# VectorE's order inside a tick of a fused Mamba and attention pipeline: product, maximum, scan instead of product, scan, maximum

## The chip, the cores and the metric

The kernel runs on one core of a Trainium2 chip. The metric is the device time of one execution, in microseconds (us). The time of the kernel before is 8423.08 us, the median of 3 runs (8422.37 to 8431.92).

The engines are called PE (TensorE, the matrix engine; PEld is its weight load), DVE (VectorE), ACT (ScalarE), POOL (GpSimd) and SP (SyncE, which here only issues DMAs). Each runs its own instructions in the order in which they are written; between engines there are only semaphores.

## The reference

Input x has 16 images of 64 channels and 64x64 points. Two layers follow each other:

```
y   = leaky_relu(conv2d_3x3(x, w1, b1));  y = leaky_relu(conv2d_3x3(y, w2, b2))
seq = y as 4096 steps of 64 channels
# Mamba: 128 inner channels d, 16 states n, steps one after the other
h   = exp(delta[d] * A[d, n]) * h + (delta[d] * u[d]) * B[n]
y[d] = sum_n h[d, n] * C[n]              # then + u*D, * silu(z), @ out_proj
# second layer, on x1 = output of the first
out_c = softmax(xc xc^T) x1              # channel attention, 64 x 64
attn  = softmax(q^T k)                   # spatial attention, 4096 x 4096 for each image
out   = x1 + w_bn [out_c ; v attn^T]
```

## The kernel before

**Stages.** The two 3x3 convolutions of all images come first. Then one pipeline carries everything else of all images. It is cut into ticks. An image has 8 chunks of 512 steps, and the 128 x 16 recurrences are packed as 16 groups of 128 lanes; one tick T is one group of one chunk, so there are 16 ticks (r = T % 16 = 0 to 15) in a chunk, 128 in an image and 2048 in all. While image a is scanned, the attention of image a-1 runs: from tick 122 on a search for the largest score (one pair of 128x512 tiles a tick), from tick 160 on the attention itself (one key tile of 128 against 1024 queries a tick, a quarter of the queries in 32 ticks).

**One tick, engine by engine.** A tick is the same number of instructions on each engine, plus what belongs to its r:
- SP fetches the `lanes` of tick T+3 (one 512 KB read from `spread_d`), after the product and `dA` of tick T-1.
- ACT: `relu` of the search difference into `gains` (line 952), which waits for the maximum of tick T-1; two `exp` into `pr` (line 1007); `dA` of tick T+1 (line 1013), which waits for `lanes` and for the scan of tick T-1; then the copies of its r.
- DVE: the *product* of lanes and B into the PSUM bank DBU (line 1141), which waits for the scan of tick T-1; the *scan* (line 1152), which waits for the product and for `dA`; the *maximum* (line 1093), one instruction that adds the PSUM bank of the search to `gains` and reduces it, and which waits for PE's search product of this tick and the relu of the tick before; then the extra instructions of its r, such as the convolution taps (r = 1, 2, 3), `ysb` (line 1133, ahead of the product of r = 3), gates and splits.
- PE: search difference (line 836), the scores (lines 899 and 901, twice), the search product for the maximum (line 836 again), the values of tick T-1 (line 911), every second tick the sums (line 926), and then the small products of its r. At r = 2 the small product is `y` (line 873): 32 matmuls that sum a whole chunk's 16 states.
- POOL: after the scan of T-1 it copies the last column into `carry` (line 1262), and after the product of T it multiplies the scanned `hst` by C (line 1269). At r = 4 it gates `ysb` (line 1275).

**Ring of banks.** All of PE's results but three take turns in 5 PSUM banks (`RING = 5`); a matmul waits until the result five uses back has been read. Four uses a tick and one for each small product. So the search product for the maximum waits for the *scores* of the tick before in a plain tick, and for the *maximum of the tick before* where one small product stands between:

```
if number[e] >= RING:
    taken(pe, sched.uses[number[e] - RING])
```

Every second chunk, at r = 11, PE transposes the row of maxima (`turn`); DVE reads it (line 1103) and splits it in three for the next quarter.

**What the change touches** is the body of DVE's loop over T. `small_use` issues the maximum; the scan's block is unchanged.

Of the kernel before, what the change touches and what calls it, by code (L numbers as in the profile page):

```python
# [92 lines left out]
def group_of(T):  # L93

    k = T % GROUPS
    return k % BLOCKS * GPB + k // BLOCKS


def slot_of(T):

    k = T % GROUPS
    return k if k >= HALVES or T // GROUPS % 2 == 0 else k + GROUPS
# [316 lines left out]
def pipeline(nc, banks, seq_d, scratch, w_in, cw, cb, w_dt_t, w_dt, dt_b, w_bc, a_log, skip,  # L419
# [4 lines left out]
    with ExitStack() as ctx:  # L424
# [138 lines left out]
        def span(j, images, tail, i):  # L563
# [9 lines left out]
            def due(name, event, times=1):  # L573

                return sched.counts.get(name, {}).get(event, 0) * times

            def wait(eng, name, event, times=1):

                if due(name, event):
                    eng.wait_ge(S[name], due(name, event, times))  # L580
# [6 lines left out]
            def bank_of(e):  # L587
                return RB[number[e] % RING]

            def full_wait(eng, e):  # L590

                if e in number:
                    eng.wait_ge(S["ring_full"], number[e] + 1)

            def taken(eng, e):

                if e in sched.freed:
                    eng.wait_ge(S[sched.freed[e][0]], sched.freed[e][1])
# [55 lines left out]
            with nc.Block() as block:  # L654
# [418 lines left out]
                def _(dve):  # L1073
                    steps = [0]

                    def link(ins):

                        steps[0] += 1
                        ins.then_inc(S["dstep"], 1)
                        dve.wait_ge(S["dstep"], steps[0])  # L1080

                    def small_use(e):
                        kind, c = e[0], e[1]
                        if kind not in DVE_USES or kind == "y":
                            return
                        full_wait(dve, e)
                        bank = bank_of(e)
                        if kind == "max":
                            k = e[2]
                            taken(dve, ("dif", c, k))  # L1090
                            if k == 0:
                                wait(dve, "max_in", sched.before(c))
                            nc.vector.tensor_tensor_reduce(  # L1093
                                out=gains[:, k % 2, :], in0=bank[:], in1=gains[:, k % 2, :], scale=1.0,
                                scalar=LOWEST, op0=ALU.add, op1=ALU.max,
                                accum_out=mxp[:, k % NT, k // NT:k // NT + 1]).then_inc(S["dve_took"], 1)
                            if k == KT - 1:
                                taken(dve, e)
                                nc.vector.tensor_reduce(mx[:], mxp[:], AX_X, ALU.max).then_inc(S["max_in"], 1)
                        elif kind == "turn":  # L1100

                            wait(dve, "nm_row", sched.before(c), 48)
                            nc.vector.tensor_scalar(nmx[:, 0, :], bank[0:NT, 0:P], -1.0, None,
                                                    ALU.mult).then_inc(S["dve_took"], 1)
                            taken(dve, e)
                            link(nc.vector.tensor_copy(nm3[:, 0, :], nmx[:, 0, :]))
                            link(nc.vector.tensor_tensor(nmx[:, 1, :], nmx[:, 0, :], nm3[:, 0, :], ALU.subtract))
                            link(nc.vector.tensor_copy(nm3[:, 1, :], nmx[:, 1, :]))
                            nc.vector.tensor_tensor(nm3[:, 2, :], nmx[:, 1, :], nm3[:, 1, :],
                                                    ALU.subtract).then_inc(S["nm3_in"], 1)  # L1110
                        elif kind == "mix":

                            nc.vector.tensor_tensor(mixw[0:CH, 0:CH], bank[0:CH, 0:CH], ident[0:CH, 0:CH], ALU.add)
                            nc.vector.tensor_tensor(mixw[CH:P, CH:P], bank[CH:P, 0:CH], ident[CH:P, CH:P],
                                                    ALU.add).then_inc(S["dve_took"], 1)
                        elif kind == "res":
                            nc.vector.tensor_tensor(accs[:], accs[:], bank[:], ALU.add).then_inc(S["dve_took"], 1)
                        elif kind == "en":
                            if c % CHUNKS == 0:
                                ins = nc.vector.tensor_copy(energy[:], bank[0:CH, 0:CH])  # L1120
                            else:
                                taken(dve, ("en", c - 1))
                                ins = nc.vector.tensor_tensor(energy[:], energy[:], bank[0:CH, 0:CH], ALU.add)
                            ins.then_inc(S["dve_took"], 1)

                    for T in range(first, last):
                        sl, r = T // GROUPS, T % GROUPS
                        ev = sched.small_uses(T)
# [6 lines left out]
                        if sched.scans(T):  # L1135
                            wait(dve, f"lanes{T % SLOTS}", T, 16)
                            if r == 0:
                                wait(dve, "ld_b", sl, 16)
                            if due("scan", T - 1):
                                dve.wait_ge(S["scan"], due("scan", T - 1))  # L1140
                            nc.vector.tensor_tensor(DBU[:], lanes[:, T % SLOTS, 1, :], bbc[:, sl % 2, :],  # L1141
                                                    ALU.mult).then_inc(
                                S["dbu_in"], 1)
                        if sched.scans(T):
                            g = group_of(T)
                            if due("dbu_in", T):
                                dve.wait_ge(S["dbu_in"], due("dbu_in", T))
                            if due("da_in", T):
                                dve.wait_ge(S["da_in"], due("da_in", T))
                            wait(dve, "carried", T - GROUPS)  # L1150
                            full_wait(dve, ("y", sl - 1 if T % GROUPS >= HALVES else sl - 2))
                            nc.vector.tensor_tensor_scan(  # L1152
                                hst[:, slot_of(T), :], dA[:, T % 2, :], DBU[:],
                                carry[:, g:g + 1] if sl % CHUNKS else 0.0, ALU.mult, ALU.add).then_inc(S["scan"], 1)
                        for e in ev:
                            if e[0] == "max":
                                small_use(e)
                        c = sl + 1
                        if sched.chunk(c):
                            x_ = xin[:, c % 2, :]  # L1160
# [168 lines left out]
```

## Time and profile before

| | us |
|---|---|
| median of 3 runs | 8423.08 |
| profiled execution, its own time | 8432.17 |
| its span, first to last instruction | 8430.3 |
| PE busy | 7658.1 (91%) |
| DVE busy | 6758.3 (80%) |
| ACT busy | 5963.6 (71%) |
| POOL busy | 3407.8 (40%) |
| granted TensorE clock, mean | 0.962 |

Busy time is summed over an engine's instructions. PE's is generous: a matmul of 512 columns is drawn as 0.38 us long, while the next one starts 0.22 us after it. So a small stall of PE can hide under a matmul's drawn end.

### The profile page before, as it was taken

The numbers are of one execution on the slowest core, as the hardware profiler recorded it, in microseconds if no ns is written. First come the engines' busy times: TensorE is split into PE (matmuls) and PEld (weight loads), VectorE is DVE, ScalarE is ACT, GpSimd is POOL, SyncE is SP. The second block draws the span as 40 slices with busy tenths as digits, with TensorE's granted clock in tenths as the row PEclk, the third lists the DMA queues.
The fourth block names the chain that finished last, engine by engine and source line by source line (L and its number), as shares of the span: only waits on it lengthen the run. The fifth ranks groups of instructions, "written<-read, shape, count | busy, mean of one in ns | idle before, by whom it ended". The sixth has DMA issues, their size and how long they took to land. (4 is left out here: it accounts for less than half of the span.)

```text
span 8430.3 us, 156342 instructions
## 1 busy us (share of the span) xinstructions
PE 7658.1 (91%) x48454; PEld 2321.5 (28%) x48454; DVE 6758.3 (80%) x10982; ACT 5963.6 (71%) x10582; POOL 3407.8 (40%) x4135
## 2 busy tenths in 40 slices
PE   8982389998999999989999999989999999989999
PEld 2220122222222222222222222222222222222222
DVE  2228889898989899888989898988989898989721
ACT  1114468777778788777877787877878787878754
POOL 0005544444444444444444444444444444434300
PEclk9985689999999999999999999999999999999999
DMA  8738878787787887877777878878787878778600
GB/s 130 121 80 217 216 202 202 196 200 186 195 206 193 201 202 197 197 190 195 197 196 198 207 191 201 200 181 201 200 201 196 201 192 206 197 183 202 150 26 11
DMA packets 886565, 1531.37 MB, mean 182 GB/s; under 512 B 409480, under 2 KB 459472, under 8 KB 885712
## 3 DMA queue, kind: packets, MB, share of 16 engines
q1 hardware_dynamic: 882640, 1520.79, 74.0%
q8 instruction: 389, 6.37, 0.4%
q14 instruction: 464, 3.80, 0.2%
q10 hardware_dynamic: 3072, 0.40, 0.0%
HBM read 1326.69 MB, written 176.95 MB: 178 GB/s over the span
## 5 line engine op out<-in xcount | busy, mean ns | idle before, releaser
L1269 POOL TENSOR_TENSOR hst<-hst,cbc 128x512 f32<-128x512 f32 x2048 | 2609.8, 1274 | 3664.6 <-DVE bank L1141 3642.7
L1152 DVE TENSOR_TENSOR_SCAN hst<-dA,carry,bank 128x512 f32<-128x512 f32 x1792 | 2293.8, 1280 | 94.7 <-ACT dA L1013 22.5
L1007 ACT ACTIVATE pr<-bank 128x512 f32<-128x512 f32 x4096 | 2226.6, 603 | 61.3 <-PE bank L901 59.1
L911 PE MATMUL bank<-pr,vt 128*32 128x512 f32 x16384 | 2192.5, 607 | 0.0
L952 ACT ACTIVATE gains<-bank 128x512 f32<-128x512 f32 x2048 | 1223.8, 598 | 1141.0 <-PE bank L836 748.8
L836 PE MATMUL bank<-s1kx,s1q 128*128 128x512 bf16 x4096 | 1588.2, 389 | 199.7 <-DMA s1kx<-kx_d 76.9
L1013 ACT ACTIVATE dA<-lanes,small 128x512 f32<-128x512 f32 x2048 | 1501.0, 733 | 354.7 <-DMA lanes<-spread_d 312.1
L899 PE MATMUL bank<-s1q,s1k 128*128 128x512 bf16 x4096 | 1568.2, 383 | 176.1 <-ACT pr L1007 152.5
L1141 DVE TENSOR_TENSOR bank<-lanes,bbc 128x512 f32<-128x512 f32 x2048 | 1514.9, 740 | 163.2 <-DMA lanes<-spread_d 56.7
L1093 DVE CUSTOM_DVE_ANT_0 gains<-bank,gains 128x512 f32<-128x512 f32 x2048 | 1369.7, 669 | 326.6 <-PE bank L836 319.2
L901 PE MATMUL bank<-t2q,t2k 128*128 128x512 bf16 x4096 | 1562.1, 381 | 0.0
L926 PE MATMUL bank<-pr,ones 128*32 128x512 f32 x8192 | 1069.5, 594 | 1.9 <-ACT dens L1022 1.7
L836 PEld LDWEIGHTS bank<-s1kx,s1q 128*128 128x128 bf16 x4096 | 397.6, 97 | 1779.5 <-issue 1137.0
L899 PEld LDWEIGHTS bank<-s1q,s1k 128*128 128x128 bf16 x4096 | 400.1, 98 | 710.1 <-ACT pr L1007 333.0
L873 PE MATMUL bank<-hst,cst 128*32 128x512 f32 x4096 | 484.4, 615 | 79.0 <-POOL hst L1269 79.0
L911 PEld LDWEIGHTS bank<-pr,vt 128*32 128x32 f32 x16384 | 323.7, 108 | 789.8 <-issue 777.4
L901 PEld LDWEIGHTS bank<-t2q,t2k 128*128 128x128 bf16 x4096 | 403.0, 98 | 403.4 <-issue 10.6
L1262 POOL COPY carry<-hst 128x1 f32<-128x1 f32 x1792 | 483.8, 270 | 40.3 <-DVE hst L1152 35.8
L926 PEld LDWEIGHTS bank<-pr,ones 128*32 128x32 f32 x8192 | 266.5, 111 | 626.2 <-issue 522.1
L388 ACT ACTIVATE biased<-bank,bias 128x512 f32<-128x512 f32 x128 | 80.9, 683 | 504.0 <-PE bank L376 504.0
L1133 DVE SCALAR_TENSOR_TENSOR ysb<-u,small,bank 128x512 f32<-128x512 f32 x128 | 95.6, 747 | 340.8 <-issue 324.7
L1152 DVE TENSOR_TENSOR_SCAN hst<-dA,bank 128x512 f32<-128x512 f32 x256 | 312.4, 1220 | 15.2 <-ACT dA L1013 5.4
(116 smaller groups left out, 5720.7 us busy)
## 6 DMA issues: line engine op xcount, KB each, us to landing
lanes<-spread_d SPq DMA_DIRECT2D x2048, 512.0 KB, 6.0
seqt<-seq_d SPq DMA_DIRECT2D x256, 128.0 KB, 4.5
spread_d<-dsp SPq DMA_DIRECT2D x128, 256.0 KB, 2.0
spread_d<-usp SPq DMA_DIRECT2D x128, 256.0 KB, 2.0
bbc<-bc_d SPq DMA_DIRECT2D x128, 256.0 KB, 3.7
cbc<-bc_d SPq DMA_DIRECT2D x128, 256.0 KB, 4.2
xpad<-in_x SPq DMA_DIRECT2D x64, 256.0 KB, 6.8
ypad<-ypad SPq DMA_DIRECT2D x128, 128.0 KB, 4.2
```

Source lines behind the costliest of these rows:

```text
L836: mm = nc.tensor.matmul(bank[:].rearrange("p (c n) -> p c n", n=HALF), s1q[:, q, nt * P:(nt + 1) * P], keys[:, 2 * mc:2 * (mc + 1), 1 if k ...
L899: nc.tensor.matmul(bank[:], s1k[:, t * P:(t + 1) * P], s1q[:, q, cols], start=True, stop=False)
L901: nc.tensor.matmul(bank[:], t2k[:, t * P:(t + 1) * P], t2q[:, q, cols], start=False, stop=True).then_inc(S["ring_full"], 1)
L911: mm = nc.tensor.matmul(ACC[CH * h + o:CH * h + o + BLOCK, :], vt[:, t, o:o + BLOCK], pr[:, T % PRING, h, :], start=t == 0, stop=t == KT - ...
L926: mm = nc.tensor.matmul(DEN[o:o + 32, :], ones[:], pr[:, (2 * p + par) % PRING, h, :], start=t == 1, stop=t == KT - 1, tile_position=(0, o))
L952: nc.scalar.activation(gains[:, k % 2, :], bank_of(e)[:], ACT.Relu).then_inc(S["act_took"], 1)
L1007: nc.scalar.activation(pr[:, T % PRING, h, :], bank_of(("S", T, h))[:], ACT.Exp).then_inc(S["p_full"], 1)
L1013: nc.scalar.activation(dA[:, (T + 1) % 2, :], lanes[:, (T + 1) % SLOTS, 0, :], ACT.Exp, scale=amat[:, g:g + 1]).then_inc(S["da_in"], 1)
L1093: nc.vector.tensor_tensor_reduce(out=gains[:, k % 2, :], in0=bank[:], in1=gains[:, k % 2, :], scale=1.0, scalar=LOWEST, op0=ALU.add, op1=A ...
L1141: nc.vector.tensor_tensor(DBU[:], lanes[:, T % SLOTS, 1, :], bbc[:, sl % 2, :], ALU.mult).then_inc(S["dbu_in"], 1)
L1152: nc.vector.tensor_tensor_scan(hst[:, slot_of(T), :], dA[:, T % 2, :], DBU[:], carry[:, g:g + 1] if sl % CHUNKS else 0.0, ALU.mult, ALU.ad ...
L1269: nc.gpsimd.tensor_tensor(h, h, cbc[:, (T - 1) // GROUPS % 2, :], ALU.mult).then_inc(S["hc_in"], 1)
```

## The change

In the body of DVE's tick the loop that issues the maximum moves from behind the scan to between product and scan. Nothing is added or removed, no wait is changed, and the instructions of PE, ACT, POOL and SP are the same in the same order.

```diff
                         if sched.scans(T):
                             ...
                             nc.vector.tensor_tensor(DBU[:], lanes[:, T % SLOTS, 1, :], bbc[:, sl % 2, :],
                                                     ALU.mult).then_inc(
                                 S["dbu_in"], 1)
+                        for e in ev:
+                            if e[0] == "max":
+                                small_use(e)
                         if sched.scans(T):
                             g = group_of(T)
                             ...
                             nc.vector.tensor_tensor_scan(
                                 hst[:, slot_of(T), :], dA[:, T % 2, :], DBU[:],
                                 carry[:, g:g + 1] if sl % CHUNKS else 0.0, ALU.mult, ALU.add).then_inc(S["scan"], 1)
-                        for e in ev:
-                            if e[0] == "max":
-                                small_use(e)
```

DVE's rows at r = 11 and the start of r = 12 of a chunk in which `turn` is read. L1141 is the product, the row into hst (L1152, or L1155 in the changed file) is the scan, and the two L1093 rows are the maximum and the read of its accumulator. Before:

```order
L1141 TENSOR_TENSOR bank5<-lanes,bbc 128x512
L1152 SCALAR_TENSOR_TENSOR hst<-dA,carry,bank5 128x512
L1093 ISA gains,mxp<-bank4,gains 128x512
L1093 ISA mxp 128x1
L1103 TENSOR_SCALAR nmx<-bank0 8x128
L1106 CAST nm3<-nmx 8x128
L1107 TENSOR_TENSOR nmx<-nmx,nm3 8x128
L1108 CAST nm3<-nmx 8x128
L1109 TENSOR_TENSOR nm3<-nmx,nm3 8x128
L1141 TENSOR_TENSOR bank5<-lanes,bbc 128x512
```

The same place now:

```order
L1141 TENSOR_TENSOR bank5<-lanes,bbc 128x512
L1093 ISA gains,mxp<-bank4,gains 128x512
L1093 ISA mxp 128x1
L1155 SCALAR_TENSOR_TENSOR hst<-dA,carry,bank5 128x512
L1103 TENSOR_SCALAR nmx<-bank0 8x128
L1106 CAST nm3<-nmx 8x128
L1107 TENSOR_TENSOR nmx<-nmx,nm3 8x128
L1108 CAST nm3<-nmx 8x128
L1109 TENSOR_TENSOR nm3<-nmx,nm3 8x128
L1141 TENSOR_TENSOR bank5<-lanes,bbc 128x512
```

The maximum has moved ahead of one scan; the rows behind the scan and the next tick's product keep their distance from this tick's product.

The second place is the end of r = 2 on DVE, where L1171 is the second convolution tap and L1133 waits for PE's `y`. Before:

```order
L1141 TENSOR_TENSOR bank5<-lanes,bbc 128x512
L1152 SCALAR_TENSOR_TENSOR hst<-dA,carry,bank5 128x512
L1093 ISA gains,mxp<-bank4,gains 128x512
L1093 ISA mxp 128x1
L1171 SCALAR_TENSOR_TENSOR cacc<-xin,small,cacc 128x512
L1133 SCALAR_TENSOR_TENSOR ysb<-u,small,bank0 128x512
```

And now:

```order
L1141 TENSOR_TENSOR bank5<-lanes,bbc 128x512
L1093 ISA gains,mxp<-bank4,gains 128x512
L1093 ISA mxp 128x1
L1155 SCALAR_TENSOR_TENSOR hst<-dA,carry,bank5 128x512
L1171 SCALAR_TENSOR_TENSOR cacc<-xin,small,cacc 128x512
L1133 SCALAR_TENSOR_TENSOR ysb<-u,small,bank0 128x512
```

What waits for PE's search product is now ahead of the scan, no longer behind it.

## Rows read from the trace of the kernel before

**Rows 1.** Page: busy time of each engine, share of the span, instructions.

```profile
PE 7658.1 (91%) x48454; PEld 2321.5 (28%) x48454; DVE 6758.3 (80%) x10982; ACT 5963.6 (71%) x10582; POOL 3407.8 (40%) x4135
```

**Rows 2.** Stretch, length; busy us of PE, PEld, DVE, ACT, POOL; granted clock; DMA.

```profile
1140.00:7960.00 6820.00, 6487.92 (x41772) 1968.98 (x41764) 6071.52 (x9915) 5388.60 (x9606) 3106.82 (x3768) 0.99 0.79 197
```

**Rows 3.** PE's waits in 1140:7960: line, releaser, us in total, times, longest.

```profile
PE bank L899 <- ACT pr L1007: 152.5, 117, 1.3
PE bank L836 <- DMA s1kx<-kx_d: 70.7, 14, 6.0
...
PE bank L836 <- DVE mxp L1093: 28.0, 58, 0.8
```

**Rows 4.** PE's longest wait in the ramp, 1000:1140 (ticks 122 to 162).

```profile
PE bank L836 <- DVE mxp L1093: 26.0, 18, 2.4
```

**Rows 5.** DVE's waits in 1140:7960.

```profile
DVE ysb L1133 <- issue: 321.1, 113, 5.5
DVE gains L1093 <- PE bank L836: 90.4, 115, 3.3
```

**Rows 6.** Line 1093 in 1140:7960: duration ns min/median/max; who waited for it.

```profile
L1093 DVE CUSTOM_DVE_ANT_0 gains<-bank,gains x1886: 661/665/694, 1141.1 to 7958.6; 128x512 f32<-128x512 f32 x189
...
  PEld bank L836: 108.5, 194
```

**Rows 7.** Timeline of DVE, r = 11 of a chunk with `turn`: start, us, engine.

```profile
4015.98 0.70 DVE L1141 TENSOR_TENSOR bank<-lanes,bbc 128x512 f32<-128x512 f32 x1
4016.71 1.28 DVE L1152 TENSOR_TENSOR_SCAN hst<-dA,carry,bank 128x512 f32<-128x512 f32 x1
4017.91 0.67 DVE L1093 CUSTOM_DVE_ANT_0 gains<-bank,gains 128x512 f32<-128x512 f32 x1
...
4018.50 0.27 DVE L1103 TENSOR_SCALAR nmx<-bank 8x128 f32<-8x128 f32 x1
```

**Rows 8.** Timeline of PE at the same place, the start of r = 12.

```profile
4017.74 0.38 PE L901 MATMUL bank<-t2q,t2k 128*128 128x512 bf16 x1
4018.64 0.39 PE L836 MATMUL bank<-s1kx,s1q 128*128 128x512 bf16 x1 [0.52 <-DVE mxp L1093]
```

**Rows 9.** Timeline of ACT at the same place.

```profile
4017.87 0.83 ACT L1065 CAST mid<-rest 64x768 bf16<-64x768 f32 x1
4018.72 0.60 ACT L952 ACTIVATE gains<-bank 128x512 f32<-128x512 f32 x1
```

**Rows 10.** Timeline of DVE, r = 1 to 3 of the next chunk.

```profile
4036.91 0.69 DVE L1093 CUSTOM_DVE_ANT_0 gains<-bank,gains 128x512 f32<-128x512 f32 x1
...
4039.29 0.70 DVE L1141 TENSOR_TENSOR bank<-lanes,bbc 128x512 f32<-128x512 f32 x1 [1.02 <-issue]
...
4045.11 0.75 DVE L1133 SCALAR_TENSOR_TENSOR ysb<-u,small,bank 128x512 f32<-128x512 f32 x1 [2.52 <-issue]
```

**Rows 11.** Timeline of PE, r = 2 of that chunk.

```profile
4040.48 1.06 PE L926 MATMUL bank<-pr,ones 128*32 128x512 f32 x8 [0.21 <-ACT dens L1022]
4041.37 3.62 PE L873 MATMUL bank<-hst,cst 128*32 128x512 f32 x32
```

**Rows 12.** Timeline of ACT, `dA` of r = 2, made in r = 1.

```profile
4039.24 0.72 ACT L1013 ACTIVATE dA<-lanes,small 128x512 f32<-128x512 f32 x1 [0.49 <-DMA lanes<-spread_d]
```

**Rows 13.** Timeline of DVE before the search, where a product directly follows a scan.

```profile
862.02 1.28 DVE L1152 TENSOR_TENSOR_SCAN hst<-dA,carry,bank 128x512 f32<-128x512 f32 x1
863.41 0.70 DVE L1141 TENSOR_TENSOR bank<-lanes,bbc 128x512 f32<-128x512 f32 x1
```

**Rows 14.** Timeline of POOL at the same place.

```profile
860.39 0.92 POOL L1262 COPY carry<-hst 128x1 f32<-128x1 f32 x1
...
863.37 0.18 POOL L1262 COPY carry<-hst 128x1 f32<-128x1 f32 x1
```

**Rows 15.** Timeline of DVE at r = 5: a slow product.

```profile
4051.47 1.39 DVE L1141 TENSOR_TENSOR bank<-lanes,bbc 128x512 f32<-128x512 f32 x1
```

**Rows 16.** Timeline of POOL at the same place.

```profile
4051.04 1.27 POOL L1275 TENSOR_TENSOR ysb<-ysb,zs 128x512 f32<-128x512 f32 x1
```

## The prediction

> **What bounds the kernel now.** I read the page first, then the busy time by stretch, the waits of each engine in the full pipeline, and last the timeline of one chunk, tick by tick. The page says PE 91%, DVE 80%, ACT 71% [rows 1]; by stretch, the full pipeline is 6820 us of 8430, and in it PE is busy 6488 us (95%) at a granted clock of 0.99, DVE 6072 us (89%) [rows 2]. Both look like a bound, so what matters is who waits for whom. PE's waits there are short: 152.5 us for ACT's exp in r = 10 of 117 chunks, 70.7 us for a load of keys once an image, and 28.0 us in 58 pieces for DVE's maximum [rows 3]. DVE's own waits are 321.1 us ahead of `ysb` in 113 chunks, which is 2.84 us each time, and 90.4 us ahead of the maximum, for PE [rows 5]. So a chunk looks like this. From `ysb` in r = 3 to about r = 15 DVE runs without a gap; from r = 15 to r = 2 PE has the small products and the 3.62 us of `y` [rows 11], and DVE waits for it, 2.52 us in the chunk shown [rows 10]. The chain that sets a chunk's length is PE's, from `y` to `y`, with short stalls in which others hold it. DVE matters where it is one of those others.
>
> **The change, part by part.** Nothing is added. In each tick from 123 on the maximum is ahead of the scan.
>
> (1) *The maximum is earlier.* Product, scan and maximum start at 4015.98, 4016.71 and 4017.91, and what follows starts at 4018.50 [rows 7]. The distances are 0.73, 1.20 and 0.59 us. Without the scan in front the maximum starts 0.6 us after the product (its own 0.70 us less the overlap that the others show) in place of 1.93: 1.3 us earlier. What was held by it on PE is seen at r = 12: the second search product needs the bank of the maximum of r = 11, because `turn` stands between them in the ring. It starts at 4018.64, right behind that maximum (4017.91 + 0.67 = 4018.58); the matmul before it started at 4017.74 [rows 7, 8]. Matmuls of this shape follow each other at 0.22 us, so PE could have gone at 4017.96, and lost 0.68 us, of which the view shows 0.52 (the drawn end of a matmul hides 0.16). With the maximum done at about 4017.3 the whole 0.68 us goes. The row for the stretch gives 28.0 us in 58 pieces [rows 3]; with the hidden 0.16 each that is 28.0 + 9.3 = **37 us**. Does it stay won? From there PE runs on its own products to `y`, and ACT's `relu` of r = 12 starts at 4018.72 because `mid` ends at 4018.70 [rows 9], so it is not what PE needs next. DVE has 2.84 us of idle time before `ysb` to let PE come 0.68 us earlier. I take it as kept.
>
> (2) *Smaller stalls of the same kind.* Weight loads of line 836 waited for the maximum 194 times [rows 6], 58 of which are the ones above. The other 136 are hidden under the drawn end of the matmul before, so each costs PE between 0 and 0.16 us: 0 to 22 us. Most stand in places where other things in PE's queue would have come next anyway; I take **8 us**.
>
> (3) *The ramp.* In ticks 122 to 160 there is a search but no attention, and DVE is the bound: PE's 26.0 us of waits for the maximum there [rows 4] are PE being early, and don't go. One lead of 1.3 us at the start of attention and some overlap in the ticks with extras may be won: 0 to 3 us, **2 us** taken.
>
> (4) *The scan is later*, by the maximum's 0.59 us where it doesn't wait, by more where it does. Who waits for a scan: ACT's `dA` of two ticks on, the product behind it, and POOL. At r = 12 and in the like ticks ACT comes to `dA` after a relu, itself released by a maximum, and two exps, three instructions of about 0.60 us [rows 9], and the scan ends 1.3 us after that maximum, so it is in time by some 0.4 us. Cost 0.
>
> (5) *DVE's own time.* Before, the product-to-scan wait was exposed (0.73 us start to start); now the maximum covers it. In exchange, in the ticks without an extra, the next product directly follows a scan that it waits for. The stretch before the search has this pair: 862.02 to 863.41, 1.39 us [rows 13], against 1.20 + 0.59 = 1.79 with the maximum between [rows 7]. A tick without extras: before 0.73 + 1.20 + 0.59 = 2.52; now 0.6 + 0.59 + 1.39 = 2.58. With extras the 1.39 is 1.20 to 1.3, and the tick is 0.1 us shorter. Together DVE stays within half a microsecond a chunk, inside its idle time. The Trainium skill says in "VectorE: DVE Perf Modes", section "The DRAIN you can't avoid", that a semaphore between Vector instructions costs nothing extra; by that, the pair would take no longer with the wait than without. The trace differs (1.39 us against 1.20), and the row is what I use; by either the sum is the same, and only the third rival becomes less likely by the page.
>
> (6) *A wait moved to the head of the queue.* In r = 15, 0 and 1 the maximum now reaches PE's product up to 1.3 us before it is there and waits, with the scan, the taps and the next product behind it. In r = 1 the maximum is at 4036.91 right behind PE both before and after; the scan (1.20) and the tap then stand ahead of the product of r = 2, which would start at about 4036.91 + 0.59 + 1.2 + 0.75 = 4039.5. In the chunk shown it started at 4039.29 because `lanes` were late [rows 10], so nothing moves; in a chunk where it starts straight behind the tap (4036.91 + 0.59 + 0.6 = 4038.1 here) it moves by 1.3 us, and `ysb`'s idle time falls from 2.84 to about 1.5 us. That is still more than the 0.68 us by which PE comes earlier. SP's fetch for r = 5 waits for this product; the chunk shown, with its product already that late, shows no stall from it up to r = 5. Cost 0, cover 0.8 us a chunk.
>
> **Sum.** 37 + 8 + 2 = 47 us, or 0.56%. Against the profiled execution's own 8432.17 us that makes 8385; that execution was 9.1 us above the median of the runs, so the predicted median is 8423 - 47 = **8376 us**.
>
> **The rivals.**
>
> *Eaten by the next wait (18%).* The 0.68 us are won at r = 12, and PE then stands 0.68 us longer at something that doesn't move with it. The candidate is r = 2: the sums wait for `dens`, 0.21 us in the chunk shown [rows 11], because ACT had to wait for the lanes of r = 2 until 4039.24 [rows 12]. These are fetched by SP behind a row of stores. Against it: in the other chunks seen the sums start with PE's own work, and the stores follow PE's products too. If it holds in every second chunk, only terms (2) and (3) are left: 8413 to 8423.
>
> *The long chain moves (6%).* If the real chain went from `ysb` through DVE to a maximum and from there through PE to `y`, each chunk would lose 1.3 us: 113 x 1.3 = 147 us, 8276. For it: DVE's gapless stretch, and that DVE's maximum does hold PE in 58 + 136 places. Against it: PE is continuous from `y` to r = 10 but for the stalls named, and the largest of these is for ACT's exp [rows 3], which no maximum holds.
>
> *Port contention, on the other side (6%).* `carry` on POOL used to run beside the maximum, and now starts together with the next product, which reads two SBUF tiles. A product does lose by a POOL instruction that runs already: 1.39 us in place of 0.70 beside POOL's 1.27 us gate [rows 15, 16]. If `carry` did that 5 times a chunk at 0.5 us and the cover of 0.8 us went, it costs (2.5 - 0.8) x 113 = 192 us less the 47: 8568. It decides from 0.16 us a tick. The rows before the search speak against it: `carry` starts at 863.37, the product at 863.41 and still takes 0.70 us, while another `carry`, in front of a product, is the one that stretches, to 0.92 us [rows 13, 14]. The Trainium skill, "SBUF — State Buffer", section "Who interferes with whom", says that a Vector instruction with two SBUF inputs and a GpSimd instruction that reads SBUF take an exclusive lock, and the one issued first blocks the other in full; by that the product could wait for the whole copy, and the gate's row agrees while the copy's does not.
>
> *Late lanes, also slower (8%).* The waits of (6) delay products, SP fetches behind products, `dA` waits for lanes, and ACT's exps stand behind `dA`. If a fetch comes 1.3 us late and nothing covers it, 113 x 1.3 - 47 = 100 us more, 8523; with half the chunks about 8450. It decides where less than 1.3 us lie between landing and `dA`. The 0.49 us wait for lanes in r = 1 [rows 12] shows that this cover is thin in one tick at least.
>
> **How the numbers follow.** Forecast, a gain of 25 to 80 us: 62%. Eaten: 18%. Long chain: 6%. The two slower ones: 14%, of which 3% come out within the bound. 0.2% is 17 us, about what a measurement can tell. Faster: 0.62 + 0.06 + 0.05 of the eaten = 0.73; slower: 0.11; same: 0.16. The likeliest case has its own range, 8343 to 8398: at the low end 37 + 22 + 3 us, and 1.3 us off each of the 14 waits for keys [rows 3] if DVE's lead brings those loads forward too, 80 us in all; at the high end the 28.0 us of the row less a few. For 8 in 10 I give 8340 to 8425: it holds the forecast and the eaten case, and leaves out the long chain and the slower ones.
>
> **What the changed profile would show.** PE's wait of line 836 for the maximum in 1140:7960 under 5 us, and the second search product of r = 12 at 0.22 us behind the scores. The wait before the maximum up from 90 to 200 us or more (3 ticks a chunk); the wait ahead of `ysb` down from 321 to 180 or so. Products at a median of 0.69 us as before, `carry` at 0.6 us or more in most ticks, where it is 0.18 us undisturbed [rows 14]. DVE's busy time the same within 1%. I am wrong if PE's 152.5 us for exp grow or if lanes waits on ACT grow by tens of us; wrong the other way if the wait for exp shrinks too.

## The result and the profile after

The changed kernel takes 8385.74 us, median of 6 runs (8380.64 to 8387.88), against 8427.73 us for the kernel before (median of 6, 8422.37 to 8431.92). The ratio is 0.995, 95% interval 0.9937 to 0.9963: 42 us faster (31 to 53), where 47 us were forecast. The predicted median was 8376 us; half of the 10 us between that and 8385.74 is the median of the kernel before, which moved from 8423.08 to 8427.73 us with three more runs. The profiled execution has a span of 8385.9 us.

The page's busy times after, to be read against [rows 1]:

```profile
PE 7640.4 (91%) x48454; PEld 2326.5 (28%) x48454; DVE 6664.7 (79%) x10982; ACT 5956.6 (71%) x10582; POOL 3789.8 (45%) x4135
```

PE's waits in the full pipeline (1140:7920; line, releaser, us in total, times, longest), which answer to [rows 3]:

```profile
PE bank L899 <- ACT pr L1007: 152.4, 117, 1.3
PE bank L836 <- DMA s1kx<-kx_d: 72.4, 14, 6.4
...
PE bank L899 <- ACT gains L952: 21.5, 62, 0.8
PE bank L926 <- ACT dens L1022: 1.1, 2, 0.6
```

The row of waits for the maximum, 28.0 us in 58 pieces before, is gone. All other rows are what they were within about 2 us. DVE's and ACT's waits in the same stretch, to be read against [rows 5]:

```profile
DVE gains L1093 <- PE bank L836: 269.0, 302, 5.2
DVE ysb L1133 <- issue: 260.9, 113, 4.4
```

```profile
ACT dA L1013 <- DMA lanes<-spread_d: 203.2, 179, 3.9
ACT dtx L993 <- PE bank L858: 183.1, 114, 1.6
```

DVE now meets PE at the maximum in 302 ticks in place of 115, and waits 178.6 us longer there in all. None of that is seen in PE's ticks 3 to 11, which keep their length within 0.1 us (table in the next section). The same place as in [rows 7] in the kernel after, r = 11 of the same chunk, on DVE:

```profile
3996.32 0.70 DVE L1141 TENSOR_TENSOR bank<-lanes,bbc 128x512 f32<-128x512 f32 x1
3997.05 0.69 DVE L1093 CUSTOM_DVE_ANT_0 gains<-bank,gains 128x512 f32<-128x512 f32 x1
3997.66 0.08 DVE L1093 DVE_READ_ACCUMULATOR2_ANT mxp<- 128x1 f32 x1
3997.66 1.28 DVE L1155 TENSOR_TENSOR_SCAN hst<-dA,carry,bank 128x512 f32<-128x512 f32 x1
3998.86 0.25 DVE L1103 TENSOR_SCALAR nmx<-bank 8x128 f32<-8x128 f32 x1
```

And on PE, the answer to [rows 8]:

```profile
3998.57 0.38 PE L901 MATMUL bank<-t2q,t2k 128*128 128x512 bf16 x1
3998.78 0.38 PE L836 MATMUL bank<-s1kx,s1q 128*128 128x512 bf16 x1
```

The second search product now starts 0.21 us behind the scores, where it was 0.90 us; PE has its 0.69 us back. The maximum ends at 3997.74, 1.04 us before PE wants its bank.

### The profile page after: what moved, and what is told of

Its sections match the earlier page's. It is cut to its first block and busy times, and to the rows that moved or that the text cites. A ratio compares the mean times of both kernels' runs of the same rounds, so it can differ in the third digit from the quotient of the medians.

```text
span 8385.9 us, 156342 instructions
## 1 busy us (share of the span) xinstructions
PE 7640.4 (91%) x48454; PEld 2326.5 (28%) x48454; DVE 6664.7 (79%) x10982; ACT 5956.6 (71%) x10582; POOL 3789.8 (45%) x4135
## 5 line engine op out<-in xcount | busy, mean ns | idle before, releaser
L1155 DVE TENSOR_TENSOR_SCAN hst<-dA,carry,bank 128x512 f32<-128x512 f32 x1792 | 2284.8, 1275 | 7.2 <-POOL carry L1262 1.1
L1093 DVE CUSTOM_DVE_ANT_0 gains<-bank,gains 128x512 f32<-128x512 f32 x2048 | 1404.8, 686 | 523.2 <-PE bank L836 499.0
L899 PE MATMUL bank<-s1q,s1k 128*128 128x512 bf16 x4096 | 1569.5, 383 | 177.4 <-ACT pr L1007 152.4
L1141 DVE TENSOR_TENSOR bank<-lanes,bbc 128x512 f32<-128x512 f32 x2048 | 1506.4, 736 | 182.4 <-DMA lanes<-spread_d 62.3
L1262 POOL COPY carry<-hst 128x1 f32<-128x1 f32 x1792 | 810.5, 452 | 868.0 <-DVE hst L1155 866.7
L1282 POOL TENSOR_TENSOR usp<-dsp,u 128x512 f32<-128x512 f32 x128 | 212.7, 1662 | 261.2 <-DVE dsp L1203 261.2
L1133 DVE SCALAR_TENSOR_TENSOR ysb<-u,small,bank 128x512 f32<-128x512 f32 x128 | 95.6, 747 | 278.8 <-issue 263.9
```

Source lines behind the costliest of these rows:

```text
L899: nc.tensor.matmul(bank[:], s1k[:, t * P:(t + 1) * P], s1q[:, q, cols], start=True, stop=False)
L1093: nc.vector.tensor_tensor_reduce(out=gains[:, k % 2, :], in0=bank[:], in1=gains[:, k % 2, :], scale=1.0, scalar=LOWEST, op0=ALU.add, op1=A ...
L1155: nc.vector.tensor_tensor_scan(hst[:, slot_of(T), :], dA[:, T % 2, :], DBU[:], carry[:, g:g + 1] if sl % CHUNKS else 0.0, ALU.mult, ALU.ad ...
```

## The experiments

Two theories stood at the start. *Bank*: all of the gain is PE's stall for the bank of the maximum of r = 11 (and a smaller one for that of r = 12). *DVE and ACT*: ticks on DVE get shorter, and ACT's relus no longer wait 335.8 us for a maximum. Each kernel is compared with the kernel before as it ran beside it, so the median of the kernel before differs by a few us from one experiment to the next.

**Where in a chunk the time goes.** A matmul's drawn end hides small stalls, so the rows of waits understate them. The starts don't. For each profiled kernel I take PE's ticks from the start of the first search product of a tick to that of the next, and add them up by r over ticks 176 to 2031 (116 chunks). The table is the difference to the kernel before, in us; minus is faster. Ticks 3, 4, 5, 8, 9 and 11 are left out: together they differ by 1.1 us at most.

| kernel | r = 6 | 7 | 10 | 12 | 13 | 14 | 15 to 2 | all |
|---|---|---|---|---|---|---|---|---|
| the change | 0.0 | 0.0 | 0.1 | -38.0 | -8.4 | 0.7 | 4.0 | -41.8 |
| e1, only r = 11 of every second chunk | 0.0 | 0.0 | 0.8 | -38.0 | 14.3 | -14.1 | 12.1 | -24.8 |
| e2, all but r = 11 and 12 | 0.0 | 0.0 | 0.1 | -22.9 | -8.4 | 0.6 | -0.4 | -31.1 |
| e3, only r = 12 | 0.0 | 0.0 | 0.0 | 0.2 | -8.4 | 4.0 | 0.6 | -3.6 |
| e4, maximum first | 1.9 | 0.0 | 0.9 | -37.2 | -8.4 | -0.1 | 57.3 | 14.5 |
| e5, delay in r = 11 | 0.0 | 0.0 | 0.0 | 57.3 | 0.3 | -1.1 | -2.3 | 54.3 |
| e6, delay in r = 5 | 15.8 | 25.0 | -15.8 | 32.2 | 0.5 | 0.1 | -0.1 | 57.9 |
| e7, `dt` first | -11.3 | 1.2 | -71.3 | -38.0 | -8.4 | 0.9 | 26.1 | -101.1 |
| e8, `dt` in the middle | 27.7 | 1.3 | -71.1 | -38.0 | -8.4 | -0.1 | 8.2 | -80.8 |
| e9, `dt` and `out` first | -11.3 | -10.6 | -102.3 | -27.3 | -8.4 | -0.1 | 30.2 | -128.9 |
| e10, e9 with the old order | 132.9 | -10.6 | -102.4 | -10.6 | -7.9 | -0.9 | -5.8 | -4.2 |
| e11, `xin` and `z` first too | -11.3 | -10.6 | -101.9 | -27.3 | -8.4 | -0.6 | 39.0 | -120.1 |

Each row is one profiled execution, so its last column need not match the median of the runs. The single columns repeat within 1 us where nothing should differ; "15 to 2" holds the waits for DMAs and scatters by some 5 us. The change gains in two places and nowhere else: at r = 12, behind the maximum of r = 11, and at r = 13, behind the maximum of r = 12.

### Only r = 11 of every second chunk

```diff
+                        early = T % (2 * GROUPS) == GROUPS + 11
                         for e in ev:
-                            if e[0] == "max":
+                            if e[0] == "max" and early:
                                 small_use(e)
                         ...
+                        for e in ev:
+                            if e[0] == "max" and not early:
+                                small_use(e)
```

> The maximum goes ahead of the scan only in tick r = 11 of every second chunk (the tick whose maximum holds PE's bank behind the transposed row), 64 of 2048 ticks; all other ticks are as before. Bank theory (the whole gain is PE's wait for that bank): about 37 us faster than before, 80% of the change's gain, and PE's row of waits for the maximum in the full pipeline falls from 28.0 us to near 0. DVE theory (the gain comes from shorter ticks and from ACT's relus no longer waiting for a maximum, 335.8 us of waits): 64 of 2048 ticks give 1 to 2 us.

8407.71 us against 8435.28, ratio 0.9968 (0.9955 to 0.998): 27 us faster, interval 17 to 38. PE's waits for the maximum in the full pipeline are down from 28.0 to 1.2 us, and ACT's waits for a maximum are as long as before:

```profile
ACT gains L952 <- DVE mxp L1093: 336.7, 528, 1.0
```

So 61 moved maxima of the 1925 that share their tick with a scan give most of what all give. (The condition names 64 ticks; three of them come after the last scan, where there is nothing to move past.) ACT's 337 us of waits are not what the change is worth: with them gone, in the change and in e2, no tick of PE gets shorter but r = 12 and 13. The stall at r = 12 goes whole, 38.0 us, as the bank theory says. What is missing to 38 is not noise alone. PE now reaches the maximum of r = 12 too early and loses 14.3 us at r = 13, which r = 14 gives back, where PE waits 6.1 us for ACT's `gains` and no longer 20.9. The ticks from r = 15 to r = 2 take 12.1 us more, of which two rows name 9.6: the sums wait 6.2 us for `dens` (1.7 before), and the loads of keys cost 75.8 us (70.7 before).

### All but r = 11 and r = 12

```diff
+                        early = r not in (11, 12)
```

(with the two loops as above)

> The complement: the maximum goes ahead of the scan in all ticks but r = 11 and r = 12. Bank theory: 0 to 5 us faster than before, the 28.0 us of PE's waits for the maximum stay, although ACT's waits for the maximum all but go. DVE and ACT theory: most of the 42 us.

8395.48 us, ratio 0.9956 (0.9942 to 0.9969): 37 us faster, interval 26 to 49. This is not what the bank theory expected, and it is not ACT either, as the first run says. PE's row has shrunk to almost nothing although neither the maximum of r = 11 nor that of r = 12 was moved inside its tick:

```profile
PE bank L836 <- DVE mxp L1093: 3.1, 9, 0.4
```

The row understates what is left. From start to start the second search product of r = 12 comes 0.42 us after the scores here, so 0.20 us of stall remain under the drawn end:

```profile
3999.45 0.38 PE L901 MATMUL bank<-t2q,t2k 128*128 128x512 bf16 x1
3999.87 0.39 PE L836 MATMUL bank<-s1kx,s1q 128*128 128x512 bf16 x1
```

Where the time comes from is seen by following DVE from `ysb` to the product of r = 11 in one chunk. Before (the same chunk as [rows 7], where that product is at 4015.98):

```profile
3988.01 0.75 DVE L1133 SCALAR_TENSOR_TENSOR ysb<-u,small,bank 128x512 f32<-128x512 f32 x1 [2.70 <-issue]
...
4014.67 1.28 DVE L1214 TENSOR_TENSOR rest<-x1c,head 64x768 f32<-64x768 f32 x1
```

In this kernel, `ysb`, then r = 11 with its old order:

```profile
3969.72 0.75 DVE L1133 SCALAR_TENSOR_TENSOR ysb<-u,small,bank 128x512 f32<-128x512 f32 x1 [2.07 <-issue]
...
3993.99 0.69 DVE L1093 CUSTOM_DVE_ANT_0 gains<-bank,gains 128x512 f32<-128x512 f32 x1 [0.29 <-PE bank L836]
...
3996.21 0.96 DVE L1218 TENSOR_TENSOR rest<-x1c,head 64x768 f32<-64x768 f32 x1
3997.20 0.70 DVE L1141 TENSOR_TENSOR bank<-lanes,bbc 128x512 f32<-128x512 f32 x1
3997.94 1.28 DVE L1156 TENSOR_TENSOR_SCAN hst<-dA,carry,bank 128x512 f32<-128x512 f32 x1
3999.13 0.67 DVE L1093 CUSTOM_DVE_ANT_0 gains<-bank,gains 128x512 f32<-128x512 f32 x1
```

It is 27.97 us before and 27.48 us here: DVE's own chain is 0.49 us shorter over eight ticks, and it is so in all 58 chunks of this kind (medians 27.97 and 27.49). Tick by tick, r = 3, 5, 6, 7 and 8 are shorter by 0.08, 0.20, 0.13, 0.12 and 0.11 us, and r = 4, 9 and 10 are longer by 0.08, 0.04 and 0.03. In r = 10 two things cancel: the maximum now waits 0.29 us for PE, and `rest` behind it is 0.32 us shorter. Before, `rest` started at 4014.67, while POOL's multiplication ran until 4015.13; now the two hardly overlap. That fits the slow product of [rows 15, 16], but no run isolates it.

In the kernel before DVE has no idle time between `ysb` and the maximum of r = 11, so the lead goes in full to the bank that PE waits for, and takes 0.49 of the 0.68 us. The table gives 22.9 us at r = 12 for it, and 8.4 us at r = 13, where the stall for the maximum of r = 12 goes in the same way: 31 us, inside the measured interval. So the order inside r = 11 makes the maximum end 1.18 us earlier and would remove the stall of 0.68 us alone; the ticks ahead of it make it 0.49 us earlier and remove most of it. The two overlap, which is why 27 and 37 us do not add to 42.

### Only r = 12

```diff
+                        early = r == 12
```

> The maximum goes ahead of the scan only in r = 12 of every chunk. There another small product stands in the ring, so the search product of r = 13 needs the bank of the maximum of r = 12; in every second chunk PE lost about 0.18 us at it. Bank theory: about 8 us faster than before (45 chunks of 0.18 us), 3 to 12. DVE theory: 128 of 2048 ticks, 2 to 3 us. Rival: less than 3 us, since PE then stands at the next wait.

8431.07 us, ratio 0.9995 (0.9986 to 1.0004): 4 us, which doesn't stand clear of no change. The times alone are inconclusive. The trace shows both the theory and the rival: r = 13 is 8.4 us shorter, the 44 small stalls of 0.18 us are gone, and r = 14 is 4.0 us longer in the same kind of chunk, since PE stands at the next wait.

### Maximum first

```diff
+                        for e in ev:
+                            if e[0] == "max":
+                                small_use(e)
                         if sched.scans(T):
                             wait(dve, f"lanes{T % SLOTS}", T, 16)
                             ...
```

> The maximum stands at the head of the tick: maximum, product, scan. Bank theory: all held banks are free at least as early as in the change, so the gain is the same 42 us, unless the wait at the head of the queue bites: PE's product for the maximum comes late in r = 15, 0, 1 and 7 to 10, and now the product stands behind it too, and SP's fetch of lanes behind the product. Theory of late lanes: a gain smaller by 20 us or more, or a loss, with ACT's waits for lanes up from 203 us.

8440.45 us, ratio 1.0005 (0.9996 to 1.0015): the whole gain is gone, although PE's waits for the maximum in the full pipeline have left the list here too. The table shows that r = 12 and 13 are as short as in the change, and that 57.3 us are lost between r = 15 and r = 2. What came in their place, on PE:

```profile
PE bank L926 <- ACT dens L1022: 20.4, 23, 1.5
PE bank L836 <- DVE mixw L1114: 8.0, 14, 0.6
```

and on ACT:

```profile
ACT dA L1013 <- DMA lanes<-spread_d: 323.4, 259, 4.8
...
ACT dA L1013 <- DVE hst L1155: 60.3, 168, 2.3
```

Part of this is the chain of the rival on late lanes: the maximum waits for PE at the head of the queue, the product behind it is late, SP's fetch waits for the product, ACT stands at `dA`, and `dens` and the sums behind it. The waits for lanes went from 203.2 us after the change to 323.4, and in all 23 places where the sums wait for `dens`, the `dA` just ahead of that copy had waited for lanes. That chain accounts for some 19 us. The loads of keys (81.4 us, 70.7 before) and `mixw` (8.0 us) add 19 us. The remaining 20 us or so are not traced, so the cause of the loss stays in part open. What is shown is that the rival is real one step further along in the order; with the product ahead of the maximum the same waits of the sums are 1.1 us.

### A delay ahead of the maximum, in r = 11 and in r = 5

```diff
+                        if sched.scans(T) and T % (2 * GROUPS) == GROUPS + 11:
+                            for h in range(2):
+                                link(nc.vector.tensor_tensor(junk[:], cst[:], cst[:], ALU.mult))
```

behind the scan of the kernel before; the second kernel has `GROUPS + 5`.

> The kernel before, with two idle multiplications of 128x256 added on DVE between scan and maximum in r = 11 of every second chunk (64 places; their result is used nowhere, and each is waited for, about 0.9 us together). Bank theory: PE loses all of it 64 times, 50 to 60 us slower than before. DVE theory (DVE has idle time ahead of ysb): no change within 5 us.

> The control: the same two idle multiplications at the same place of the tick, but in r = 5 of every second chunk, where the maximum holds ACT's relu but no bank that PE is about to need. Bank theory: no change within 5 us beyond what DVE's later ticks carry on to r = 11. There DVE is without a gap from r = 3 on, so the delay of 0.9 us travels to the maximum of r = 11 and costs PE the same 50 to 60 us. A theory in which only the tick's own order counts: 0.

In r = 11: 8485.4 us against 8433.62, ratio 1.0062 (1.0048 to 1.0076), 52 us slower. In r = 5: 8490.26 us, ratio 1.0066 (1.0052 to 1.008), 56 us slower. From the scan to the maximum behind it 2.16 us pass in place of 1.20, so each delay is 0.96 us; of the 64, 61 stand in a tick that has a maximum, and 61 of 0.96 us are 59. So DVE's time at 80% busy, with 2.84 us of idle time in each chunk, is worth its full price at both places tried between `ysb` and the maximum of r = 11. PE's rows, first for r = 11, then for r = 5:

```profile
PE bank L837 <- DVE mxp L1094: 85.3, 58, 1.8
```

```profile
PE bank L837 <- DVE mxp L1094: 75.1, 118, 1.1
...
PE bank L859 <- DVE u L1185: 13.4, 58, 0.5
```

85.3 - 28.0 = 57.3 us in the same 58 places: the delay arrives whole, and the table has the same 57.3 us at r = 12. With the delay in r = 5 it doesn't travel to r = 11 whole, as was expected. PE pays 15.8 us at `dt` in r = 6, which waits for the later `u`, 25.0 us at r = 7 for the maximum of r = 6 (59 of the 118 places), and only 32.2 us at r = 12; r = 10 gives 15.8 us back. The size was right, the way was another.

### ACT's stall of r = 10, the largest that is left

After the change ACT waits 1.6 us in each chunk for the product `dt` of r = 6 (183.1 us), and PE waits 1.3 us in r = 10 for the exps of r = 9 (152.4 us). Before the change ACT's wait for `dt` was 53.1 us; now that ACT hardly waits for maxima, it is there earlier. Two kernels, e7 and e8, move `dt` forward in PE's queue. In e7:

```diff
             plan += [e for e in uses if e[0] == "max"]
+        plan += [e for e in uses if e[0] == "dt"]
         if self.attends(T - 1):
             plan.append(("PV", T - 1))
```

and DVE makes `u` at the head of r = 5; in e8 `dt` is between `PV` and `SUM` and `u` stays.

> On top of the change: the product dt of r = 6 stands ahead of the values and the sums in PE's queue (1.9 us earlier), and DVE makes u at the head of r = 5 instead of its end, so that it is ready. ACT waits 1.6 us for dt in each chunk after the change (183.1 us), and from there to its exps of r = 9 it is busy without a gap, which PE then waits for in r = 10 (152.4 us). If that chain is the largest stall left: 100 to 165 us faster than the change. If something else holds ACT or PE as soon as this goes: under 50 us.

> On top of the change: dt of r = 6 stands between values and sums in PE's queue (0.97 us earlier), u is unchanged. If ACT's wait for dt is the start of the chain: 60 to 110 us faster than the change, about 0.9 us in each of 117 chunks. Otherwise under 20 us.

For e7 8327.53 us, ratio to the kernel before 0.987 (0.9854 to 0.9885), and for e8 8351.97 us, 0.9904 (0.9889 to 0.9919). Against the change (0.995) that is 0.8% and 0.5% faster, some 67 and 39 us: less than expected in both. PE's drawn wait fell only by a third, though r = 10 is 71 us shorter from start to start in both. In e7 26 us are lost again between r = 15 and r = 2, and in e8 `dt` in the middle makes r = 6 itself 28 us longer. In e7 ACT's wait had moved one copy on, to the product `out` of r = 7:

```profile
PE bank L900 <- ACT pr L1008: 101.2, 117, 0.9
```

```profile
ACT x1c L996 <- PE bank L869: 66.3, 119, 1.6
```

### out moved too, with either order on DVE

Kernel e9 is e7 with `out` beside `dt` (`e[0] in ("dt", "out")`). Kernel e10 is e9 with DVE's old order, and so measures what the order is worth there. Kernel e11 is e9 with `xin` and `z` moved as well.

> On top of e7_dt_first: the product out of r = 7 also stands ahead of values and sums in PE's queue. In e7 ACT's wait moved from dt to the copy of out (66.3 us in 119 chunks), and PE's wait for exp in r = 10 is still 101.2 us. If it is the same chain: another 50 to 65 us, that wait falls to 35 to 50 us. DVE is the limit of this: PE comes to the bank of the maximum of r = 11 up to 1.5 us earlier than after the change, and there were 1.04 us of room (maximum ends 28.91 us after ysb, PE wants it at 29.95), so waits for the maximum come back, at most 0.4 us in every second chunk, 25 us. If another wait is right behind: under 20 us.

> e9 with DVE's old order (product, scan, maximum). Bank theory: what the order is worth grows with what is taken off PE's chain before r = 12. In the kernel before PE lost 0.68 us at r = 12; now it comes up to 1.5 us earlier, so it loses up to 2.2 us in one half of the chunks and about 1.5 in the other: 100 to 190 us slower than e9, with PE's waits for the maximum above 80 us. If the order is worth the same 42 us whatever stands before: 42 us slower than e9.

> On top of e9: the products xin and z of r = 0 also stand ahead of values and sums. ACT waits for xin 158 to 183 us in all these kernels. PE isn't held by ACT in r = 0 and 1, it is the bound there, so the chain theory says no gain: within 10 us of e9. If every wait of ACT counted: 50 us or more.

| kernel | median us | ratio to before | interval |
|---|---|---|---|
| dt, out first; product, maximum, scan | 8296.03 | 0.9838 | 0.9824 to 0.9851 |
| the same; product, scan, maximum | 8438.44 | 1.0007 | 0.9998 to 1.0016 |
| dt, out, xin, z first; product, maximum, scan | 8305.37 | 0.9848 | 0.9834 to 0.9861 |

By the ratios e9 is 27 us faster than e7, less than the 50 to 65 expected; PE's wait for exp is 70.0 us, and ACT waits for the maximum again (66.6 us in 155 places). Of the 38.0 us at r = 12, 10.7 come back as waits for the maximum. Kernel e9 beats both kernels of this study, by 1.6% and 1.1%. Moving `xin` gives nothing, as expected, although ACT's 140 us of waits for it all but vanish; its waits for lanes grow from 328.7 to 426.0 us.

Kernel e10 is the test of the bank theory: the same edit of DVE's order that was worth 42 us is worth 142 us here. The size lies in the expected 100 to 190 us, but by another way, so that is luck. At r = 12 PE loses less than in the kernel before, not more. It loses 144 us in r = 6, at `dt`. That product always takes the bank of the maximum of r = 5, and now it asks for it ahead of the values and the sums. With the old order, on DVE and then on PE:

```profile
3997.97 0.67 DVE L1094 CUSTOM_DVE_ANT_0 gains<-bank,gains 128x512 f32<-128x512 f32 x1
```

```profile
3998.70 1.12 PE L859 MATMUL bank<-u,wdt 128*128 128x512 f32 x2 [0.99 <-DVE mxp L1094]
```

and its sum over the pipeline:

```profile
PE bank L859 <- DVE mxp L1094: 114.7, 117, 1.3
...
PE bank L837 <- DVE mxp L1094: 16.7, 54, 0.4
```

With the new order the maximum of r = 5 ends before PE is there, and `dt` follows the search product by 0.21 us:

```profile
3943.37 0.38 PE L837 MATMUL bank<-s1kx,s1q 128*128 128x512 bf16 x1
3943.58 1.02 PE L859 MATMUL bank<-u,wdt 128*128 128x512 f32 x2
```

## Why the prediction was right

**The bound.** PE's chain with short stalls, and DVE relevant only where PE waits for its result: shown, since all that the change, e1, e2 and e3 do to PE's ticks is at r = 12 and 13 and behind. The two delays show at what price, and e10 shows that the price depends on how early PE comes, at `dt`.

**Term 1, the bank of r = 11: right, 37 us forecast.** The stall of 0.68 us is gone, row and all, and r = 12 is 38.0 us shorter in the change and in e1 alike; e1 as a whole gives 27 us (17 to 38), because other ticks give some of it back. That "what was held by it on PE is seen at r = 12" is shown in the rows above.

**Term 2, 8 us.** The trace gives 8.4 us, all at r = 13 (44 chunks, 0.18 us each before). The 8 was picked from a range of 0 to 22 without knowing the place, so the close hit is partly luck. For the rest of the 136 loads the table shows nothing.

**Term 3, the ramp, 2 us.** PE's waits for the maximum there fell from 26.0 us [rows 4] to 16.6, where the forecast said that they don't go. Tick 176 is reached 2.7 us earlier, but the other kernels scatter there by 3 us, so what it is worth stays open.

**Term 4, the later scan, cost 0: right.** No wait of ACT for a scan appears in the full pipeline after the change; they do (60.3 us) when the maximum is first.

**Term 5, DVE's own time, priced at 0: this was the weak step.** The parts were right: after the change a tick without extras is 2.59 us and not 2.52 (r = 4, from product to product, 3972.60 to 3975.19 below), and one with extras is about 0.1 us shorter. The conclusion "inside its idle time" was wrong. All of DVE's idle time is ahead of `ysb` and in the ticks around it; between `ysb` and r = 11 there is none, so the 0.49 us gained there are worth 31 us by themselves in the trace of e2, and 37 us (26 to 49) in its time. The forecast survived by luck: the same stall had already been credited in full to term 1.

```profile
3972.60 0.69 DVE L1141 TENSOR_TENSOR bank<-lanes,bbc 128x512 f32<-128x512 f32 x1
3973.20 0.68 DVE L1093 CUSTOM_DVE_ANT_0 gains<-bank,gains 128x512 f32<-128x512 f32 x1
...
3973.81 1.27 DVE L1155 TENSOR_TENSOR_SCAN hst<-dA,carry,bank 128x512 f32<-128x512 f32 x1
3975.19 1.32 DVE L1141 TENSOR_TENSOR bank<-lanes,bbc 128x512 f32<-128x512 f32 x1
```

The wait for the scan shows in the last two rows: 1.38 us from scan to product, against 1.39 us in [rows 13].

**Term 6, the wait at the head.** The wait before the maximum went to 269 us (200 or more forecast). The wait ahead of `ysb` fell from 321.1 to 260.9 us, not to 180: 0.5 us a chunk where I had allowed for 1.3. Why it fell less wasn't looked into by a run. The ticks from r = 15 to r = 2 are 4.0 us longer after the change, which is within their scatter, so cost 0 stands.

**Rivals.** *Eaten*: not here; in e1, with r = 11 alone, some 12 us are. *Long chain*: no; but a part of it is true, since the leads of DVE's ticks do reach PE. *Port*: the product's time didn't grow, and `carry` is what waits. POOL's busy time rose from 3407.8 to 3789.8 us, and the median of `carry` in the pipeline from 183 to 562 ns (39% of them at 600 or more, where "most" was forecast), with no price in PE's ticks. On POOL, in the tick of the rows above:

```profile
3972.10 0.62 POOL L1262 COPY carry<-hst 128x1 f32<-128x1 f32 x1 [0.49 <-DVE hst L1155]
```

The Trainium skill, "SBUF — State Buffer", section "Who interferes with whom", says that the one issued first blocks the other; by that rule the trace agrees here, as DVE's tap (from 3971.95) came before the copy. The tap ended at 3972.68 and the copy at 3972.72. *Late lanes*: my sign of it, ACT's waits for lanes growing "by tens of us", did appear (145.6 to 203.2 us) with no loss. The sign was badly chosen: what counts is PE's wait for `dens`, 1.1 us after the change and 20.4 us where the maximum is first. DVE's busy time was to stay within 1% and fell by 1.4%; the last section says why.

## What to carry to other kernels

In an engine that is 80% busy, ask where its idle time lies: between its last wait and the moment at which somebody needs its result it may have none, and there every tenth of a microsecond counts, in an early tick as in a late one, until the result comes early enough. Order the instructions of a tick by who waits for them: what holds a ring's bank goes early, what only its own engine needs goes late, and what a DMA fetch waits for stays ahead of anything that can itself wait (the last is shown by one kernel, whose loss is explained in part). A stall can hide under a drawn matmul, so compare starts, tick by tick: that found the 8 us at r = 13 which the rows of waits don't have. And price an order again after every other edit: the same one was worth 42 us, and 142 us once two of PE's products had moved forward in its queue.

## What the hardware showed that was not expected

A 1-column copy on POOL (`carry`) takes 0.18 us undisturbed and 0.62 us when it starts behind a DVE instruction with two SBUF inputs. The DVE instruction isn't slowed (0.73 us). The maximum, which has one input in PSUM and one in SBUF, rose from a median of 665 ns [rows 6] to 685 ns after the change, in a stretch of nearly 1900 of them:

```profile
L1093 DVE CUSTOM_DVE_ANT_0 gains<-bank,gains x1887: 671/685/694, 1143.2 to 7919.0; 128x512 f32<-128x512 f32 x189
```

Its start-to-start time to the next instruction went from 0.59 to 0.61 us. Why it rose wasn't followed up. DVE's busy time fell by 1.4% all the same (6758.3 to 6664.7 us), with the same instructions. The page counts time in which two drawn instructions overlap once, so its busy time is not the sum over an engine's instructions. Their durations add up to 7284.2 us before and 7254.2 us after: 30 us net are shorter instructions, with 21 in `rest` alone (1384 to 1220 ns on average), and the other 64 us are more overlap.
